# Router logits from attention rows and folded weights, with top-2 selection beside the last layer norm

## The reference

```
h = _L0_tok_ref(0, x, ...)                    # relu(x W0) * (x W1), then Wo
h = _layernorm(h + _L0_attn_ref(h, ...))      # window of 64 to either side
h = _layernorm(h + _L0_ffn_ref(h, ...))       # quantised gate/up/down, I = 1024
h = _layernorm(h + _L1_attn_ref(h, ...))      # causal; attn @ Wo.T + bo
h = _layernorm(h + _L1_ffn_ref(h, ...))       # mixture of 8 experts
```

```
scores = jax.nn.softmax(x @ wg, axis=-1)      # wg: 256 x 8
gates, idx = jax.lax.top_k(scores, k)         # k = 2
masks = jax.nn.one_hot(idx, E)
counts = masks.sum(0)
loc = jnp.cumsum(masks, 0) - 1 + offsets[None]
pos = jnp.where(keep, idx * C + loc_sel, E * C)
buf = zeros.at[pos.reshape(-1)].set(xk)       # rows go to their two experts
```

## Time and profile before

| what | value |
|---|---|
| median of three runs | 926.13 us |
| the profiled execution itself | 926.73 us |
| span in its trace | 924.6 us |
| PE busy | 834.7 us, 90% |
| DVE, ACT, POOL busy | 495.4, 433.1, 376.6 us |
| mean granted TensorE clock | 0.951 of full |
| steps 0 to 255 (scores of the attention) | 51 to 547 us of the span |
| expert part | about 597 to 880 us |

### The profile page before, as it was taken

How to read it: one execution, slowest core, us unless ns; L and a number is a source line. 1 busy time by engine, 2 the same in 40 slices (tenths; PEclk the granted TensorE clock), 3 DMA queues, 4 the chain that set the end, 5 groups by cost and what they waited for, 6 DMA issues and landing times.

```text
span 924.6 us, 14104 instructions
## 1 busy us (share of the span) xinstructions
PE 834.7 (90%) x4796; PEld 536.8 (58%) x4796; DVE 495.4 (54%) x1899; ACT 433.1 (47%) x792; POOL 376.6 (41%) x549
## 2 busy tenths in 40 slices
PE   6999999899899899899999997699999999999920
PEld 2665546556556455355545454277787787787820
DVE  5675344779788798788768764231131230220246
ACT  1525335688787787888566664132202202112005
POOL 6336224656465373253483635701231221220423
PEclk9999999999899899999899999799999999999975
DMA  9662021212202220210332206420423523512342
GB/s 344 218 232 75 25 70 30 60 53 70 71 7 65 70 55 18 70 47 25 110 99 64 72 31 234 144 75 9 145 50 111 149 27 128 153 19 62 40 108 91
DMA packets 58662, 81.47 MB, mean 88 GB/s; under 512 B 8160, under 2 KB 52193, under 8 KB 56160
## 3 DMA queue, kind: packets, MB, share of 16 engines
q1 hardware_dynamic: 49232, 70.22, 23.6%
q0 software_dynamic: 7296, 9.47, 6.0%
q10 hardware_dynamic: 2064, 0.90, 0.4%
HBM read 35.37 MB, written 19.68 MB: 60 GB/s over the span
## 4 chain that ended last, share of the span: by engine, by line
PE 76%; DVE 11%; issue 4%; ACT 4%; POOL 3%; DMA 1%; SPq 0%; POOLq 0%; ACTq 0%; DVEq 0%
PE ps L1572 15%; PE ps L1586 15%; PE ps L959 6%; PE ps L908 6%; PE ps L1005 5%; PE ps L870 5%; PE ps L892 4%; DVE junk L1159 4%; PE ps L1031 3%; PE ps L976 3%; PE ps L1014 3%; PE ps L925 2%; PE ps L935 2%; ACT probs L683 1%; PE ps L1041 1%
## 5 line engine op out<-in xcount | busy, mean ns | idle before, releaser
L1159 DVE CUSTOM_DVE_ANT_0 junk<-ps,maskb 128x256 bf16<-128x256 f32 (+4 forms) x512 | 200.2, 435 | 82.6 <-PE ps L870 82.1
L683 ACT ACTIVATE probs<-ps 128x512 f32<-128x512 f32 (+1 forms) x304 | 156.9, 551 | 61.0 <-PE ps L892 58.9
L1613 ACT ACTIVATE hTe<-ps,qs 128x640 f32<-128x640 f32 x64 | 50.8, 794 | 218.8 <-PE ps L1572 218.8
L1520 POOL DMA_INDIRECT mixed_rows<-ysb,ids x40 | 62.1, 1553 | 221.4 <-DVE ysb L1688 218.4
L1586 PE MATMUL ps<-ks,hTe 128*128 128x256 f32 x640 | 143.3, 379 | 0.0
L1572 PE MATMUL ps<-dxT,qs 128*128 128x320 f32 x512 | 140.1, 433 | 1.2 <-DVE dxT L1666 1.2
L1586 PEld LDWEIGHTS ps<-ks,hTe 128*128 128x128 f32 x640 | 119.3, 190 | 15.1
L1572 PEld LDWEIGHTS ps<-dxT,qs 128*128 128x128 f32 x512 | 96.7, 190 | 40.5 <-DVE dxT L1666 0.9
L870 PE MATMUL ps<-ks,qs 96*128 96x256 bf16 (+4 forms) x512 | 106.5, 291 | 3.8 <-DVE nmax L1159 2.0
L892 PE MATMUL ps<-qs,ks 99*128 99x256 bf16 (+4 forms) x512 | 103.6, 288 | 6.5 <-DVE nmax L1159 3.5
L908 PE MATMUL ps<-probs,vaug 128*32 128x256 f32 (+4 forms) x1024 | 89.3, 422 | 6.5 <-ACT oT L692 3.3
(11 more groups left out here) (199 smaller groups left out, 1244.3 us busy)
## 6 DMA issues: line engine op xcount, KB each, us to landing
qs<-parts SPq DMA_DIRECT2D x96, 128.0 KB, 2.4
ks<-parts SPq DMA_DIRECT2D x96, 128.0 KB, 2.4
qs<-w SPq DMA_DIRECT2D x8, 1024.0 KB, 9.6
ks<-w SPq DMA_DIRECT2D x8, 1024.0 KB, 4.9
dispatched_rows<-att SPq DMA_DIRECT2D x8, 650.0 KB, 10.9
ks<-dispatched_rows SPq DMA_DIRECT2D x4, 650.0 KB, 7.4
x_sb<-xT SPq DMA_DIRECT2D x8, 256.0 KB, 4.0
mixed_rows<-h SPq DMA_DIRECT2D x4, 512.0 KB, 3.1
```

What stands on the lines that cost most here:

```text
L683: act.activation(probs_of(u)[:, heads[0]:heads[-1] + 1, :], turned_bank((u, half, i))[:, 0:len(heads) * w].rearrange("p (j n) -> p j n", n=w),
L1159: ins = dve.tensor_tensor_reduce(out=junk[:, b - (b > V_BANK), a * (hi - lo):(a + 1) * (hi - lo)], in0=score_bank((u, half, i))[:, a * (hi ...
L1520: pool.indirect_dma_start(out=acc, out_offset=bass.IndirectOffsetOnAxis(ap=ids[:, e, t:t + 1], axis=0), in_=ysb[:, e % 2, t, :], in_offset ...
L1613: act.activation(hTe[:, e % 2, m, :].rearrange("p (a n) -> p a n", a=2), ps[:, 2 * (n % 2):2 * (n % 2) + 2, 0:HC], ACT.Silu, bias=b1s[:, e ...
```

## The change

1. **New phase `gset`** (parts at steps 46 to 49). The gate weights are centred on the chip (the column mean is taken out), so that the mean of a row needs no correction. The second layer's output weights are loaded a second time, in another layout (`wot`, 256 KB), into `x_sb`, whose use has ended; PE multiplies them by the centred gate to the folded gate `fold` (256 x 8) and makes the gate of the output bias in the same group.
2. **New phase `hg`** (steps 112, 144, 176, 210, each right behind the `qkv` of its batch): the residual rows, which stand turned in `actT`, times the centred gate. DVE adds the bias part and keeps the result in `own`.
3. **`gate`** has one part: the turned attention rows, which `o` parts 0 and 1 leave in `actT`, times `fold`; DVE adds `own`. The second turning (eight transposes, two ACT copies for each batch) is gone, and so is the mean's correction (`gsum`). It stands at steps 184, 215, 247 and 280, beside `o` part 2.
4. **`route`**: its scaled logits get a tile of their own (`exps_of`, before a part of `sel`); the count moves from part 4 to 3, POOL's scaling from 2 to 3, ACT's exponentials from 3 to 4, and the rest of DVE's work with them; the wait for the exponentials comes last. For the last batch, `gate` 3 and `route` 3 start at step 280 (from 282 and 284) and stand ahead of `o` 7 (step 278) in the table.
5. **`send`** waits for the normed rows tile by tile.

```diff
-    ("o", 3, 150), ("ffn", 3, 157), ("qkv", 6, 162), ("o", 4, 182), ("gate", 0, 186), ("route", 0, 188),
-    ("send", 0, 196), ("qkv", 7, 196), ("o", 5, 213), ("gate", 1, 217), ("route", 1, 219), ("send", 1, 228),
-    ("o", 6, 245), ("gate", 2, 258), ("route", 2, 260), ("send", 2, 270), ("o", 7, 278), ("gate", 3, 282),
-    ("route", 3, 284), ("send", 3, 293),)
+    ("o", 3, 150), ("ffn", 3, 157), ("qkv", 6, 162), ("gset", 0, 46), ("hg", 0, 112),
+    ("hg", 1, 144), ("hg", 2, 176), ("hg", 3, 210), ("o", 4, 182), ("gate", 0, 184), ("route", 0, 188),
+    ("send", 0, 196), ("qkv", 7, 196), ("o", 5, 213), ("gate", 1, 215), ("route", 1, 219), ("send", 1, 228),
+    ("o", 6, 245), ("gate", 2, 247), ("route", 2, 260), ("send", 2, 270), ("gate", 3, 280),
+    ("route", 3, 280), ("o", 7, 278), ("send", 3, 293),)
...
@@ SP, dense @@
+                    if phase == "gset" and c == 0:
+                        sp.wait_ge(*d_full(("tok", B - 1, f"u{ME - 1}")))
+                        sp.dma_start(x_sb[:, :, 0:D], wot).then_inc(wot_in, 16)
...
@@ POOL, dense, send @@
                         if c == 0:
                             pool.wait_ge(routed, i + 1)
-                            pool.wait_ge(ln_done, NORMED["o", B + i] + NT)
...
+                        if k == 0:
+                            pool.wait_ge(ln_done, NORMED["o", B + i] + t + 1)
...
@@ ACT, dense @@
-                    if phase == "gate" and c == 0:
-                        for k in range(2):
-                            turned_pair(("gate", i, f"T{k}"), k)
-                    if phase == "route" and c == 3:
+                    if phase == "route" and c == 4:
...
@@ PE @@
+                def by_expert(key, weights):
+
+                    o = d_open(key)
+                    for t in range(NT):
+                        for k in range(KD):
+                            ins = mm(o[:, t * E:(t + 1) * E], actT[:, k, t * P:(t + 1) * P], weights[:, k, :],
+                                     start=(k == 0), stop=(k == KD - 1))
...
-                        if c == 0:
-                            for k in range(2):
-                                pe.wait_ge(*d_out(("o", B + i, f"p{k}")))
-                                turn_pair(("gate", i, f"T{k}"), att[:, (B + i) % 2, :, :], k)
...
+                        for k in range(2):
+                            pe.wait_ge(*d_out(("o", B + i, f"a{k}")))
+                        by_expert(("gate", i, "lg"), fold)
+                    if phase == "hg":
...
+                        by_expert(("hg", i, "hg"), gatew)
+                    if phase == "gset" and c == 0:
+                        pe.wait_ge(*d_out(("bias", 1, "one")))
+                        o = d_open(("gset", 0, "s"))
+                        for k in range(KD):
+                            mm(o[:, 0:E], ones, gatew[:, k, :], start=(k == 0), stop=(k == KD - 1))
+                        for k in range(KD):
+                            ins = pe.transpose(o[:, (k + 1) * P:(k + 2) * P], ar[1][:, k * P:(k + 1) * P], ident)
...
+                    if phase == "gset" and c == 2:
+                        pe.wait_ge(wot_in, 16)
+                        pe.wait_ge(gate_set, 1)
+                        pe.wait_ge(*d_out(("gset", 0, "s")))
+                        o = d_open(("gset", 0, "w"))
+                        for m in range(KD + 1):
+                            for k in range(KD):
+                                src = x_sb[:, k, D:D + P] if m == KD else x_sb[:, k, m * P:(m + 1) * P]
+                                ins = mm(o[:, m * E:(m + 1) * E], src, gatew[:, k, :], start=(k == 0),
+                                         stop=(k == KD - 1))
...
@@ DVE, route, c == 0 @@
-                        dve.wait_ge(mean_turned, ROOTS["o", B + i])
-                        then(dve.tensor_tensor(rt[:, :, :], gsum[:, :].rearrange("p (o e) -> p o e", o=1).to_broadcast(
-                            [P, NT, E]), wide(mv[:, :, 0]), ALU.mult))
-                        dve.wait_ge(*d_full(("gate", i, "lg")))
-                        dve.tensor_tensor(cur, lg[:, 0:NT * E].rearrange("p (t e) -> p t e", e=E), rt[:, :, :],
-                                          ALU.add).then_inc(d_out(("gate", i, "lg"))[0], 1)
...
@@ DVE, dense @@
+                    if phase == "gate":
+                        key = ("gate", i, "lg")
+                        dve.wait_ge(*d_full(key))
+                        dve.tensor_tensor(low[:, :, 0:E], dense_bank(key)[:, 0:NT * E].rearrange(
+                            "p (t e) -> p t e", e=E), own[:, i, :, :], ALU.add).then_inc(d_out(key)[0], 1)
+                    if phase == "hg":
+                        key = ("hg", i, "hg")
+                        dve.wait_ge(*d_full(key))
...
```

More of the change, by code:

```diff
@@ L128, in dense_units @@
     if phase == "gate":
-        return (("T0", "T1"), ("lg",))[c]
+        return ("lg",)
+    if phase == "hg":
+        return ("hg",)
+    if phase == "gset":
+        return (("s",), (), ("w",), ())[c]
     if phase == "route":
-        return ("cnt",) if c == 4 else ()
+        return ("cnt",) if c == 3 else ()
     if phase in ("bias", "wq"):
@@ L169 @@
 T_LAST, AT, USES, FREE_AT = {}, {}, [0] * BANKS, [(-100, 0)] * BANKS
[L170 removed]
+READ_LATER = {"tok": {"h": 1}, "ffn": {"u": HIDDEN}, "gate": {"l": 0}, "gset": {"s": 1, "w": 1}, "hg": {"h": 0}, "route": {"c": 1}, "bias": {"o": 0}}
 def take(kind, n, key, later=0, part=1):
@@ L253, in build @@
         sel = sb("sel", [P, NT, 3, E])
-        exps_of = sel[:, :, :, :].rearrange("p t k e -> p (t k e)")[:, 0:NT * (E + 1)].rearrange("p (t e) -> p t e", t=NT)
+        exps_of = sb("exps_of", [P, NT, E + 1])
+        fold = sb("fold", [P, KD + 1, E])
+        own = sb("own", [P, B, NT, E])
         past = sb("past", [P, NT, 2, E])
@@ L1078, in dense @@
+                    if phase == "route" and c == 3:
                         pe.wait_ge(chosen, i + 1)
@@ L1243, in route @@
                                           ALU.is_equal).then_inc(chosen, 1)
-                    if c == 5:
-                        dve.wait_ge(raised, i + 1)
-                        link(5, dve.tensor_reduce(tiles[:, :, D + 1], pp[:, 0, :, :], AX.X, ALU.add))
+                    if c == 4:
                         dve.wait_ge(*d_full(cnt))
@@ L1268, in route @@
                         then(dve.tensor_tensor(past[:, :, :, :], past[:, :, :, :], mk[:, 0:NT, :, :], ALU.mult))
-                        then(dve.tensor_reduce(loc[:, :, :], past[:, :, :, :], AX.X, ALU.add))
+                        link(5, dve.tensor_reduce(loc[:, :, :], past[:, :, :, :], AX.X, ALU.add))
+                    if c == 6:
+                        linked(5)
+                        dve.wait_ge(raised, i + 1)
+                        then(dve.tensor_reduce(tiles[:, :, D + 1], pp[:, 0, :, :], AX.X, ALU.add))
                         dve.tensor_copy(posu[:, i, :, :], loc[:, :, :]).then_inc(routed, 1)
@@ L1361, in dense @@
                             variances(0, NT)
+                    if phase == "gate":
[3 more added lines that the diff above has]
+                            "p (t e) -> p t e", e=E), own[:, i, :, :], ALU.add).then_inc(d_out(key)[0], 1)
+                    if phase == "hg":
+                        key = ("hg", i, "hg")
+                        dve.wait_ge(*d_full(key))
+                        dve.wait_ge(*d_out(("gset", 0, "w")))
+                        dve.tensor_tensor(own[:, i, :, :], dense_bank(key)[:, 0:NT * E].rearrange(
+                            "p (t e) -> p t e", e=E), fold[:, KD:KD + 1, :].to_broadcast([P, NT, E]),
+                            ALU.add).then_inc(d_out(key)[0], 1)
+                    if phase == "gset" and c == 1:
+                        key = ("gset", 0, "s")
+                        dve.wait_ge(*d_full(key))
+                        for k in range(KD):
+                            ins = dve.scalar_tensor_tensor(gatew[:, k, :], dense_bank(key)[:, 0:E], -1.0 / D,
+                                                           gatew[:, k, :], ALU.mult, ALU.add)
+                        ins.then_inc(gate_set, 1)
+                        dve.tensor_copy(x_sb[:, :, D:D + P], dense_bank(key)[:, P:(KD + 1) * P].rearrange(
+                            "p (k n) -> p k n", k=KD)).then_inc(d_out(key)[0], 1)
+                    if phase == "gset" and c == 3:
+                        key = ("gset", 0, "w")
+                        dve.wait_ge(*d_full(key))
+                        dve.tensor_copy(fold[:, :, :], dense_bank(key)[:, 0:(KD + 1) * E].rearrange(
+                            "p (k e) -> p k e", e=E)).then_inc(d_out(key)[0], 1)
                     if phase == "route":
```

38 lines of the change are left out of this document (14 added, 24 removed).

## The result

The changed kernel takes **949.27 us** (median of 5 runs, 943.47 to 950.16), the kernel before 926.13 (925.48 to 928.57): 1.024 times as long [1.0217, 1.026], slower. The forecast was 940.0 in a range of 930 to 947. The sign was right, the time lies 2 us above the range. The profiled execution is the 943.47 one, span 941.3 us, which lies inside the range; the other four took 948.8 to 950.2. What lies between these two times is the first thing that the experiments look at.

What follows compares the result with a forecast made beforehand. TensorE was taken as the bound, with 76% of the chain of waits. Terms 2.05 + 6.4 + 2.5 + 4.8 - 1.8 - 1.4 + 0.5 + 0.9 gave +13.9 on 926.73, less 0.6: 940.0 us, range 930 to 947.

Steps and rivals of the forecast that it cites:

- The fold, clock: Behind PE's wait for `wot`: PE comes back at half clock for 3.4 to 5.8 us, +2.5 us.
- The fold: Steps 40 to 56, the new `gset` phase: PE's work, its wait for `wot` and half clock, +10.95 us together.
- the wait: Step 48: PE idles for `wot`, issued behind twelve `qkv` 2 DMAs, +6.4 us (bounds 5.5 and 7.4).
- the work: `gset`: column sums, two transposes and twelve passes, all on PE's chain, +2.05 us.
- The four `hg` groups: Steps 112, 144, 176, 210: 0.7, 1.2, 1.2 and 1.7 us, together +4.8 (bounds 2 and 6.9).
- Gate 0: Batch 0 loses eight transposes, the column sums and two DVE operations: -1.8 us.
- gate 2: Moves from step 258 to 247: +1.8 us at the new place, -1.3 at the old, net +0.5.
- Gate 1: Batch 1 loses 1.02 us on PE and 0.4 of DVE operations: -1.4 us.
- The tail: Last batch, attention end to posu: logits ahead of output products, DVE late, +0.9 us (bounds -1.8 and +1.5).
- The two products take 3.5 from there at full clock: Last batch's output products: 3.5 us after the logits end at 571.5, ending at 575.0 us.
- Rival B: Whole kernel: every addition shows, plus short PSUM waits; about +20 us, 946 us and above; chance 12%.
- Rival C: Faster: selection runs under output products, `wot` issued before 159 us, `hg` hidden; -0.5 to -2.3 us, 923.8 us; chance 3%.

Runs made afterwards that it cites:

- experiment 3: Kernel before plus only the load of `wot` at the change's place and PE's wait for it, nothing reading it: 934.39 us, ratio 1.0078.
- the execution of 948.27: The profiled execution, 948.27 us, when the unedited changed kernel was measured again.
- experiment 2: Changed kernel with the load of `wot` issued at the start of `qkv` 2 (step 38), ahead of its twelve DMAs: 936.84 us, ratio 1.0098.
- experiment 7: experiment 2 without the four `hg` groups, zero added for the residual part, so routing differs: 930.48 us, ratio 1.0024.
- experiment 8: experiment 7 with the last batch's logits and selection moved behind its output products: 927.44 us, ratio 0.9981.
- experiment 9: Changed kernel, complete, with `wot` loaded from step 38 and the last batch's logits and selection behind its output products: 934.46 us, ratio 1.0077.
- experiment 4: Kernel before with only the four `hg` groups added, results copied to SBUF and unused: 934.55 us, ratio 1.0082.
- experiment 10: experiment 9 with the logits of batches 1 and 2 at the old gates' steps, 217 and 258: 931.33 us, ratio 1.0044.
- experiment 1: Changed kernel again, no edit, for a second profile: median 943.54 us, ratio 1.0188.
- experiment 6: Changed kernel with 22 filler matmuls of 512 columns on PE ahead of its wait for `wot`: 943.05 us, ratio 1.0171.

## Why the prediction was wrong, point by point

**The step that failed** is that the sum took the falls of the clock outside the stall as fixed. Its only term for the clock is "The fold, clock"; the clock of the tail was read off the profile before, and everywhere else a changed fall stands at nothing. The runs show falls that come elsewhere, longer or shorter, in every kernel and in two executions of the same one: -4.2 us in layer 0, +2.0 around batch 1, 6.66 us instead of 3.5 for the two products of the tail, and some 6 us between the traced execution and the median. The points below give each.

**The fold** was right in mechanism and place, and its size came out by luck: 10.95 forecast, 10.7 measured. Within it the wait was 5.57 (forecast 6.4; SP issued at 164.8 and not 166.3, since its twelve issues took 7.7 us and not 8.9), the work 1.9 (2.05), and the rest, the clock, 3.3 (2.5, with 2.9 as the upper end). The Trainium skill's page "DMA: Bandwidth & Descriptors", section "Issuing engines are not separate DMA queues", calls the time to initiate a DMA usually small relative to the DMA itself. For one DMA that is not far off here (0.60 us of issue, 2.4 from issue to landing for a `parts` DMA). For a burst it is no guide: twelve issues take 7.7 us against 3.3 for the landing of the load behind them, and moving one issue ahead of them is worth 8.8 us of PE's time.

**Layer 0 behind the stall** had no term: -4.2 in the trace of 943.47, and the same in experiment 3. It is not a fixed gain of the stall: the execution of 948.27 has 1.3 of it, and experiment 2 has 2.3 with no stall. In the traced execution it made the change look better than my sum.

**The four `hg` groups**, +4.8 forecast, are the mis-sized term: 5.7 at their places, 6.4 to 7.3 in medians (experiments 2 and 7, 8 and 9, and 4). "Of that ACT can hide some 0.5" was right for `hg` 1 and 2 (1.24 and 1.32). "0.7, where DVE is the slower" for `hg` 0 was wrong: 1.40. The rest lies where falls of the clock moved and, in experiment 4, where PE waits for DVE behind one.

**Gates.** Gate 0 was -1.3 for -1.8, gate 2 +0.5 for +0.5. Gate 1 was +1.3 for -1.4. "The logits themselves only move by a few steps within PE's chain: 0" holds: the 1.7 at the new place appears in full, and the old place gives as much back where the fall there is of the same length (experiment 10). With the 6.8 us of low clock that the kernel before has there, gate 1 is -0.7 (experiment 8, half of what I had); the other 2.0 are the fall of 10.2 us in its place.

**The tail**, +0.9 forecast, +2.1 measured. The logits took 2.3 us for 2.7. "The two products take 3.5 from there at full clock" failed: 6.66, as the clock fell at 584.2 with PE busy. DVE, on the other hand, was not late for the second residual sum (it had waited 0.32 for it), so the root started 2.9 behind the products and not 4.0.

**The range** failed for a reason that no term held. Taken one by one, the misses against the trace of 943.47 add up to +2.8. The other 6 us up to the median are the second time of the same program, with 17 us more at half clock in the trace of experiment 1. I took the low clock as something that follows an idle time, and its falls elsewhere as fixed. They are neither: they move with every shift, and between two executions of one program. A term of zero with bounds of about -4 to +6, my estimate from the stretches above, belonged in the sum. That the first measurement's median fell on the upper time, and not on 943.54 as in experiment 1, is chance. Rival B, with "946 and above", came nearest in number; it was not its mechanism. Its stall of 7.4 was 5.57 and its `hg` of 6.9 was 5.7 at the places; the tail (2.1 for 1.5) and the clock at the fold (3.3 for 2.9) passed its prices, and the short PSUM waits it named are not what separates the two times.

**Rival C's** point of decision, the load issued in time, was reached in experiment 2 and the kernel was still slower; it needed the `hg` groups hidden as well, and no place that I tried hides them. No complete version beat the kernel before; the best, experiment 10, is 0.4% slower.

## What to carry to other kernels

An algebraic saving must be counted in passes at their price on the chip: sixteen extra 8-column passes for a batch (1.7 to 1.9 us) cost twice the eight transposes (0.89) that they save. A load that a new step needs is issued where its queue is empty, ahead of a stage's burst of issues and not behind it. Where PE sets the pace, give the sum a term for falls of the clock that move, and compare several executions before a few microseconds are put down to an edit.

## What the runs showed of the hardware that I had not expected

The granted clock of TensorE falls from 2.4 to 1.2 GHz not only after idle time. It did so with PE busy for 6.80 of 6.80 us (584.2 in the change, 441.1 before) and right behind a filled stall (172.3 in experiment 6). Its places differ between executions of one program, which gave two separate times, 943.4 and 949 us, with 91 and 108 us at half clock. Behind a stall of 6 us the falls of the next 150 us were sometimes shorter: before, the three falls from 181.7 to 311.3 hold 20.4 us at half clock, and in experiment 3 the three from 251.0 to 315.8 hold 10.2, but the three behind the stall of the 948.27 execution (193.0 to 322.7) hold 17.0. Why, no run here shows. The size of it is not small: with the logits of batch 1 at one step, steps 208 to 240 cost from 1.5 us less to 2.3 more than before, as the low clock in them went from 3.4 to 13.7 us.
